# A transformer tower's batch loop on one core: the inner loop over eight experts written out

## The reference

```
h = embedding(x) @ W_e2h + b, then 6 times: conv over 3 taps to 256 channels, a * sigmoid(g), (glu + x) * 0.7071
h = h @ W_h2e + b
h = h + attention(layernorm(h)):  8 heads of 16; two score maps, softmax(q1 k1) and softmax(q2 k2);
      statistics of windows of 4 rows of both maps (mean, std, max, min) -> small MLP -> alpha;
      out = (alpha * attn1 + (1 - alpha) * attn2) @ v, then @ Wo
h = h + ffn(layernorm(h)):  layernorm, x_attn = normed @ attn_w.T + b + x;
      tok = x_attn.reshape(2, 8, 1024, 128); expert e: gelu(tok[:, e] @ fc1[e] + b) @ fc2[e] + b; gelu(y @ next_w.T + b)
```

## Time and profile before

| | |
|---|---|
| median of 3 runs | 6209.45 us (6199.03 to 6216.81) |
| profiled execution | 6212.76 us, span of its instructions 6210.8 us |
| instructions in the span | 116943 |
| first batch's loop body starts (first score maximum) | 137.8 us |
| last batch's body starts | 5722.6 us |
| mean granted TensorE clock | 0.932 of full speed |

### The profile page before, as it was taken

The page is one execution under the profiler, slowest core; times in us unless marked ns, Lnnn a source line. Parts: engine busy times, 40 slices in busy tenths (PEclk is TensorE's granted clock), DMA queues, the critical chain, the costliest instruction groups (busy, mean ns, idle before and its releaser), DMA issues.

```text
span 6210.8 us, 116943 instructions
## 1 busy us (share of the span) xinstructions
PE 5360.9 (86%) x34070; PEld 2471.5 (40%) x34070; DVE 5117.9 (82%) x5665; ACT 5197.9 (84%) x7937; POOL 2442.0 (39%) x4439
## 2 busy tenths in 40 slices
PE   6988989889898988989889898988989889898985
PEld 4443424334243443424334243443424334243442
DVE  1988889888888988889888888888889888888982
ACT  2988888889897888888889897888889889897984
POOL 6524344342433424344342433424344342433422
PEclk8999999999998999999999998999999999998996
DMA  1001010010101001010010101001010010101000
GB/s 37 19 21 27 17 30 19 20 27 23 25 20 29 19 21 27 18 29 19 20 27 23 25 20 29 17 22 27 18 29 19 21 26 23 26 20 28 19 20 12
DMA packets 165050, 142.09 MB, mean 23 GB/s; under 512 B 89196, under 2 KB 108268, under 8 KB 164140
## 3 DMA queue, kind: packets, MB, share of 16 engines
q1 hardware_dynamic: 159100, 124.09, 8.6%
q0 software_dynamic: 4352, 8.92, 0.7%
q10 hardware_dynamic: 816, 0.02, 0.0%
HBM read 21.26 MB, written 8.91 MB: 5 GB/s over the span
## 4 chain that ended last, share of the span: by engine, by line
PE 56%; issue 13%; DVE 12%; ACT 9%; POOL 4%; SPq 2%; another core or an unknown queue 1%; DMA 1%; ACTq 0%; DVEq 0%; POOLq 0%
PE ps_w L386 22%; PE ps_o L386 12%; PE ps_t L386 12%; PE ps_s L386 11%; DVE rowmin L712 6%; ACT junk L575 4%; DVE negmax L707 3%; SPq L328 2%; ACT exps L581 1%; DVE bn L724 1%; ACT hpre L630 1%; DMA kst<-part 1%; DVE o_raw L720 1%; ACT stage L585 1%
## 5 line engine op out<-in xcount | busy, mean ns | idle before, releaser
L707 DVE TENSOR_REDUCE negmax<-ps_s 128x1 f32<-128x1024 f32 x2048 | 2490.8, 1216 | 855.6 <-PE ps_s L386 752.8
L575 ACT ACTIVATE junk<-ps_s,negmax 128x1024 bf16<-128x1024 f32 x2048 | 2295.4, 1121 | 282.4 <-DVE rowmin L712 272.0
L712 DVE TENSOR_REDUCE rowmin<-ps_s 128x1 f32<-128x1024 f32 x2048 | 2485.5, 1214 | 0.0
L581 ACT ACTIVATE exps<-ps_t 128x1024 f32<-128x1024 f32 x2060 | 2122.3, 1030 | 373.7 <-PE ps_t L386 239.6
L386 PE MATMUL ps_s<-kst,qst 96*128 96x512 bf16 x4096 | 1305.0, 401 | 540.5 <-ACT junk L575 448.3
L386 PE MATMUL ps_o<-exps,v_cur 128*32 128x256 f32 x16512 | 1391.9, 411 | 155.8 <-DVE o_raw L720 126.6
L386 PE MATMUL ps_t<-qst,kst 99*128 99x512 bf16 x4120 | 1315.7, 403 | 83.8 <-ACT exps L581 69.1
L386 PE MATMUL ps_w<-xc,cw 128*128 128x256 f32 x4704 | 1182.2, 388 | 0.0
L386 PEld LDWEIGHTS ps_w<-xc,cw 128*128 128x128 f32 x4704 | 918.4, 196 | 218.6 <-issue 12.6
L850 POOL TENSOR_SCALAR ctmp<-ug 128x256 f32<-128x256 f32 x408 | 164.6, 403 | 1610.2 <-ACT ug L650 1594.8
L386 PEld LDWEIGHTS ps_s<-kst,qst 96*128 96x128 bf16 x4096 | 344.6, 100 | 1133.4 <-ACT junk L575 812.2
(11 more groups left out here) (179 smaller groups left out, 3903.4 us busy)
## 6 DMA issues: line engine op xcount, KB each, us to landing
qst<-part SPq DMA_DIRECT2D x1542, 32.0 KB, 2.0
kst<-part SPq DMA_DIRECT2D x1542, 32.0 KB, 2.0
qst<-mrow SPq DMA_DIRECT2D x1028, 1.5 KB
out_dram<-z SPq DMA_DIRECT2D x17, 512.0 KB, 3.2
fc1s<-in_fc_w SPq DMA_DIRECT2D x17, 256.0 KB
fc2s<-in_fc_w SPq DMA_DIRECT2D x17, 256.0 KB
cw<-in_conv_w SPq DMA_DIRECT2D x1, 2304.0 KB
odif<-in_table,idx POOLq DMA_INDIRECT x136
```

What stands on the lines that cost most here:

```text
L575: nc.scalar.activation(junk[:, n % 2, :], ps_s[:, n % 2, :], ACT.Exp, bias=negmax[:, r, t:t + 1], accum_out=sumsq[:, r, t:t + 1]).then_inc ...
L581: nc.scalar.activation(exps[:, n % RING, :], ps_t[:, :, :].rearrange("p c q -> p (c q)"), ACT.Exp, scale=0.5).then_inc(s_exp, 1)
L707: nc.vector.tensor_reduce(negmax[:, r, t:t + 1], ps_s[:, n % 2, :], axis=AX, op=ALU.max, negate=True)\
L712: nc.vector.tensor_reduce(rowmin[:, r, t:t + 1], ps_s[:, n % 2, :], axis=AX, op=ALU.min)\
```

## The change

On every engine the inner loop over `e` becomes a Python loop, so the body stands eight times in the code, and the only hardware loop left is the one over `group`, which runs twice. `i = group * E + e` now has a register and a constant in it. In DVE's and POOL's streams `pos.update(n=0)` begins each copy of the body at the same chain count. Nothing else is changed: the same tasks in the same steps on the same engines.

```diff
-            with sp.Fori(0, NB // E) as group, sp.Fori(0, E) as e:
-                i = group * E + e
-                sp.wait_ge(s_emb, i * (16 * T) + 16 * T)
-                settle()
-                load_ids(i + 1)
-                load_expert("body", i, e)
-                for j in range(U):
...
+            with sp.Fori(0, NB // E) as group:
+                for e in range(E):
+                    i = group * E + e
+                    sp.wait_ge(s_emb, i * (16 * T) + 16 * T)
+                    settle()
+                    load_ids(i + 1)
+                    load_expert("body", i, e)
+                    for j in range(U):
...
-            with pe.Fori(0, NB // E) as group, pe.Fori(0, E) as e:
-                i = group * E + e
-                for n in range(STEPS):
-                    scores(i, n)
-                    weighted(i, n)
-                    scores_t(i, n)
-                    for tk in STEP[n]:
-                        task("body", i, tk)
+            with pe.Fori(0, NB // E) as group:
+                for e in range(E):
+                    i = group * E + e
+                    for n in range(STEPS):
+                        scores(i, n)
+                        weighted(i, n)
+                        scores_t(i, n)
+                        for tk in STEP[n]:
+                            task("body", i, tk)
...
-            with dve.Fori(0, NB // E) as group, dve.Fori(0, E) as e:
-                i = group * E + e
-                for n in range(STEPS):
+            with dve.Fori(0, NB // E) as group:
+                for e in range(E):
+                    i = group * E + e
+                    pos.update(n=0)
+                    for n in range(STEPS):
```

More of the change, by code:

```diff
@@ L356, in _ @@
             load_unit(0)
-            with sp.Fori(0, NB // E) as group, sp.Fori(0, E) as e:
-                i = group * E + e
-                sp.wait_ge(s_emb, i * (16 * T) + 16 * T)
-                settle()
-                load_ids(i + 1)
-                load_expert("body", i, e)
-                for j in range(U):
[L365 to L368, removed]
-                    settle()
-                    store_mrow("body", i, j)
-                    if j + 1 in (U // 2, U):
-                        wait_side(sp, "body", i, "pool", QK[(j + 1) % U // H][-1])
-                        settle()
-                    load_unit((j + 1) % U)
-                    if ("gelu2",) in sum((STEP[n] for n in range(j * T, j * T + T)), []):
-                        store_out("body", i)
+            with sp.Fori(0, NB // E) as group:
+                for e in range(E):
+                    i = group * E + e
+                    sp.wait_ge(s_emb, i * (16 * T) + 16 * T)
+                    settle()
+                    load_ids(i + 1)
+                    load_expert("body", i, e)
+                    for j in range(U):
+                        if j:
+                            sp.wait_ge(s_st, i * STEPS + T * (j - 3) + T + LAG_T)
+                        else:
+                            sp.wait_ge(s_exp, i * STEPS + 1)
+                        settle()
+                        store_mrow("body", i, j)
+                        if j + 1 in (U // 2, U):
+                            wait_side(sp, "body", i, "pool", QK[(j + 1) % U // H][-1])
+                            settle()
+                        load_unit((j + 1) % U)
+                        if ("gelu2",) in sum((STEP[n] for n in range(j * T, j * T + T)), []):
+                            store_out("body", i)
             load_expert("tail", NB, 0)
@@ L677, in _ @@
                 task("pre", 0, tk)
-            with act.Fori(0, NB // E) as group, act.Fori(0, E) as e:
-                i = group * E + e
-                for n in range(STEPS):
[L681 to L684, removed]
+            with act.Fori(0, NB // E) as group:
+                for e in range(E):
+                    i = group * E + e
+                    for n in range(STEPS):
+                        exp_t(i, n)
+                        for tk in STEP[n]:
+                            task("body", i, tk)
+                        squares(i, n)
             for n in range(LAG_T):
@@ L821, in _ @@
             pos.update(loop=True, base=pos["n"], n=0, per=3)
-            with dve.Fori(0, NB // E) as group, dve.Fori(0, E) as e:
[L823 to L828, removed]
+            with dve.Fori(0, NB // E) as group:
+                for e in range(E):
+                    i = group * E + e
+                    pos.update(n=0)
+                    for n in range(STEPS):
+                        row_max(i, n)
+                        row_min(i, n)
+                        for tk in STEP[n]:
+                            task("body", i, tk)
             assert pos["n"] == pos["per"], pos
@@ L1004, in _ @@
             pos.update(loop=True, base=pos["n"], n=0, per=per)
[L1005 to L1009, removed]
+            with pool.Fori(0, NB // E) as group:
+                for e in range(E):
+                    i = group * E + e
+                    pos.update(n=0)
+                    for n in range(STEPS):
+                        for tk in STEP[n]:
+                            task("body", i, tk)
             assert pos["n"] == pos["per"], pos
```

## The result

The changed kernel takes **6164.59 us** (median of 5 runs, 6161.53 to 6170.18), the kernel before beside it 6209.45 us (5 runs, 6193.15 to 6216.81). The ratio is 0.9935, with a 95% interval of 0.9922 to 0.9948: 40 us less by the ratio, 45 by the medians. The profiled execution took 6161.53 us (span 6159.6), 51.2 us less than the profiled one of before.

A forecast was written before the change was run, and what follows sets the result against it. The prediction took unit 0's load to bound the batch boundary, with branch stalls of PE and ACT hidden behind it and SP's uncovered. Its terms, 29 + 14 = 43 us, taken from 6212.8, gave 6170 us, range 6140 to 6200.

The forecast's parts named there:

- What bounds the boundary: At the batch boundary, PE's and ACT's branch stalls are hidden behind unit 0's load, for which PE waits 3.7 us each.
- Part 1: Load of unit 0 at 14 boundaries: without the jump's instruction packets it gains 2.1 us each, 29 us.
- Part 2: SP issues the next `idx` copy earlier, so POOL's gathers start earlier; first eight steps 1.0 us shorter at 14 boundaries, 14 us.
- Only the load gets shorter: At the batch's start, Part 2 gives nothing because the steps behind the earlier pause stay as late; 6184 us, chance 0.13.
- The branch stall in full: At the boundary PE's fetch holds the load up, so 3.8 us comes back each, plus Part 2; 6146 us, chance 0.16.
- Lost at a fixed wait: Some steps into the batch, the boundary's gain is waited for again, but for 0.5 us; 6206 us, chance 0.13.
- Straight code stalls elsewhere: In the written-out bodies, late fetches stall engines 3.8 us each; with 20 exposed, 6246 us; chance 0.05.

The follow-up runs named there:

- two bodies per trip: Kernel before with two bodies written out per trip of an inner loop of 4, on all engines: 6074.41 us against 6095.69, ratio 0.9966.
- PE alone: Kernel before with only PE's eight bodies written out, the other engines keeping nested loops: 6082.22 us against 6095.69, ratio 0.9977.
- all but SP: Kernel before with PE, ACT, DVE and POOL written out, SP keeping its loops: 6077.62 us (ratio 0.9973) without the pause, 6172.21 (0.9944) with it.
- the last comparison: Changed kernel, SP alone, all but SP, and loops kept with early `idx`, against the kernel before (6207.87 us): ratios 0.9936, 0.9966, 0.9944, 0.9967.
- SP alone: Kernel before with only SP's eight bodies written out: 6083.61 us (ratio 0.9984) on the chip without the pause, 6187.04 (0.9966) on one with it.

## Why the prediction was right, and where not

**What bounds the boundary**: right by the rows, with less margin than I gave it. The load landed last at the boundaries of before, but PE's branch stall stood 0 to 1.6 us behind it in line, and where the load was a little shorter (between the passes of the changed kernel, all seven jumps of two bodies per trip) it was the last. The other engines' stalls were hidden: with all four kept (PE alone) the gap is 4.2 us, as in the changed kernel.

**Part 1, 14 x 2.1 = 29 us**: the size was right and a little low. The load fell from 11.3 to 9.4 us, in the forecast's measure (from the first `kst` copy) to 8.7, where 10.7 - 2.1 = 8.6 was expected; PE's wait fell to 1.6 us where 1.5 stood; all but SP gave 35 us (25 to 45). The attribution was half right. I read nearly the whole excess of 2.4 us as the jump's packets and let an ordinary fetch come in at 0.3, one load in three. Before, every load met one: two bodies per trip showed that about 0.9 of the excess was an ordinary fetch of PE at an unlucky fixed place, which straight code spreads over 4 loads of 14. On the chip without the pause the load got as short and the time followed by half only.

**Part 2, 14 x 1.0 = 14 us**: the mechanism stands as far as SP's stall, the late gathers and the first steps that get shorter when they start earlier. Alone it is worth 21 us (12 to 29), the first eight steps fell by 0.9 and 1.3 us. Its addition to part 1 was taken for granted, and that step was too simple: in the traces little of it is left on top of part 1, which gave a few us more than its term. The two errors cancel, which is why 6170 lies 5 us from 6164.59; that closeness is luck. How the pause and the low clock around it turn an earlier gather into fewer us I haven't shown, and the clock, which the forecast left out, rose with every edit of the last comparison.

**Rivals.** *Only the load gets shorter* (6184) is nearest to what the split shows, but its number is 20 us too high. *The branch stall in full* (6146) fell as a sum: the boundary gave back 2.2 us, not 3.8; but its mechanism has a share, as the second in line. *Lost at a fixed wait* (6206) fell on the chips with the pause: the distance of two batches follows, 372.3 to 368.9. On the one without it, with SP's loop kept, something like it seems to take back half of the gap's gain. *Straight code stalls elsewhere* fell: PE waits no longer on issue in the middle of the batch than it did, and without any loop the kernel isn't slower. The rule of the Trainium skill (Runtime: NRT & Kernel Launch, Instruction fetch mechanics), that a taken branch out of the held pages waits for its fetch, holds here on each of the engines, and the trace agrees at both ends: 3.95 us at the one PE branch left, and none at the 14 that went; before, the jumps took 3.6 to 4.5 us on PE, and on ACT, DVE, POOL and SP the loop's head came 2.4 to 3.3 us behind the branch. It doesn't say what the saving is: here 2.2 us of PE's 3.8, since a copy on the path stood beside the fetch.

## What to carry to other kernels

Before you cost a loop's jump, look at what releases each engine after it: here three of five stalls of 2.4 to 4.5 us (ACT's, DVE's and POOL's) were covered; what paid was a load on the path that shared its DMA engines with the fetched code, with PE's own stall close behind it, and one queue (SP) whose stall stood ahead of a chain of copy, gather and pause. Such a chain can be had without the unrolling: moving a copy of 4 KB off the batch's start gave half of the gain with the loops kept, and 15 us more on top of the change. And a mean over boundaries hides the kind: two bodies per trip put both kinds side by side in one trace.

## What the runs showed of the hardware

- The pause near the gathers' end, in which ACT and DVE are released by nothing that the profile shows (mostly 4 to 7 us a batch), went with the chip and not with the kernel: none of the four traces from one chip has it (19.5 to 19.9 us for eight steps), all ten from elsewhere do (25.1 to 27.6), SP alone and all but SP are among both, and the kernel before takes 6096 us there and 6205 to 6209 elsewhere. What makes it is open. A comparison of kernels across chips would have been off by 110 to 114 us, more than twice the effect.
- One instruction packet of 16 KB lengthens the issue of a copy that it meets from 0.59 to between 0.9 and 1.95 us: in the trace of before, 92 of the 96 such packets that meet a unit's copies do, and only 3 of the 95 slow copies have none beside them. The last landing of a load goes from 1.95 to between 2.5 and 4.0 us where the loop head's packets meet it. The 8 KB packets of the four other engines didn't lengthen the mean load with PE written out alone (9.3 us); single landings took up to 2.3 us there, and 2.45 to 2.84 at two boundaries of the changed kernel.
